# Causal attention block: softmax sums by additions of the weighting exponentials, maxima from high parts alone

## What is computed

```
x = x + 0.5 * (LN(x) @ sign_weight^T * scale + bias)        # feed-forward, ternary weights
x = x + softmax_causal(K Q^T / sqrt(32)) V @ Wo + bo        # 16 heads of 32, on LN(x)
x = x + 0.5 * (LN(x) @ sign_weight^T * scale + bias)        # feed-forward again
```

## Time and profile before

| | us |
|---|---|
| median of 3 runs | 1121.8 (1120.65 to 1125.34) |
| the profiled execution | 1119.35 |
| its span | 1117.6 |
| PE busy in the span | 1069.2 |
| ACT, DVE, POOL busy | 921.3, 738.3, 343.9 |
| granted TensorE clock, mean | 0.984 of full |

### The profile page before, as it was taken

The page is one execution under the profiler, slowest core; times in us unless marked ns, Lnnn a source line. Parts: engine busy times, 40 slices in busy tenths (PEclk is TensorE's granted clock), DMA queues, the critical chain, the costliest instruction groups (busy, mean ns, idle before and its releaser), DMA issues.

```text
span 1117.6 us, 26124 instructions
## 1 busy us (share of the span) xinstructions
PE 1069.2 (96%) x9472; PEld 692.7 (62%) x9472; DVE 738.3 (66%) x2306; ACT 921.3 (82%) x2577; POOL 343.9 (31%) x471
## 2 busy tenths in 40 slices
PE   5799999999999999999999999999999999999896
PEld 3576655565666665666666666665666666664465
DVE  6866577787535766889645776789744676755344
ACT  2269998999989989879988988878988988989641
POOL 3841232233002413445201323435301332300343
PEclk8898999999999999999999999999999999999899
DMA  6463211021104120421113211421112211000111
GB/s 203 155 217 124 96 50 40 3 78 50 34 8 154 31 68 30 152 69 50 37 34 107 68 48 50 143 78 46 44 40 86 73 63 50 22 21 12 42 65 38
DMA packets 42015, 77.71 MB, mean 70 GB/s; under 512 B 5536, under 2 KB 11680, under 8 KB 41888
## 3 DMA queue, kind: packets, MB, share of 16 engines
q1 hardware_dynamic: 41888, 76.04, 20.4%
HBM read 49.81 MB, written 25.17 MB: 67 GB/s over the span
## 4 chain that ended last, share of the span: by engine, by line
PE 77%; ACT 12%; DVE 5%; POOL 2%; issue 2%; DMA 1%; SPq 0%; ACTq 0%; DVEq 0%; POOLq 0%
PE bank L1134 31%; PE bank L1255 10%; PE bank L1193 10%; PE bank L1227 10%; PE bank L1156 8%; ACT masked_scores L1034 7%; ACT prob L1060 4%; PE bank L1145 3%; PE bank L1235 3%; DVE st L820 1%; DVE masked_scores L870 1%; POOL xt L730 1%; DMA xt<-in_L_attn_x_dram 1%; PE bank L1208 1%; DVE hn L839 1%
## 5 line engine op out<-in xcount | busy, mean ns | idle before, releaser
L870 DVE CUSTOM_DVE_ANT_0 masked_scores<-bank,mask 128x512 f32<-128x512 f32 (+3 forms) x768 | 379.6, 554 | 222.1 <-PE bank L1193 221.0
L1034 ACT ACTIVATE masked_scores<-masked_scores,mst 128x512 f32<-128x512 f32 (+3 forms) x768 | 467.5, 619 | 2.0 <-DVE mst L870 2.0
L1060 ACT ACTIVATE prob<-bank 128x512 f32<-128x512 f32 (+1 forms) x640 | 301.7, 558 | 58.0 <-PE bank L1235 56.9
L769 POOL TENSOR_SCALAR_AFFINE_SELECT prob<-prob 128x512 f32<-128x512 f32 (+1 forms) x96 | 78.6, 819 | 365.5 <-ACT prob L1060 364.8
L1134 PE MATMUL bank<-hT,wqk 128*128 128x512 f32 x768 | 190.5, 397 | 0.0
L1227 PE MATMUL bank<-qT,kT 32*128 32x512 f32 (+2 forms) x2304 | 173.0, 376 | 4.9 <-DVE mst L870 1.9
L1193 PEld LDWEIGHTS bank<-kT,qT 32*128 32x128 f32 x2304 | 94.7, 184 | 117.1 <-issue 52.4
L1193 PE MATMUL bank<-kT,qT 32*128 32x512 f32 (+2 forms) x2304 | 161.9, 376 | 4.7 <-ACT prob L1060 3.8
L1134 PEld LDWEIGHTS bank<-hT,wqk 128*128 128x128 f32 x768 | 140.6, 188 | 36.9 <-ACT prob L1060 7.2
L1034 ACT ACTIVATION_READ_ACCUMULATOR masked_scores<-masked_scores,mst 128x1 f32 x768 | 155.8, 203 | 0.0
L1227 PEld LDWEIGHTS bank<-qT,kT 32*128 32x128 f32 x2304 | 99.5, 184 | 72.0 <-issue 47.0
(11 more groups left out here) (87 smaller groups left out, 971.2 us busy)
## 6 DMA issues: line engine op xcount, KB each, us to landing
wqk<-weight_scratch SPq DMA_DIRECT2D x30, 512.0 KB, 3.3
wvo<-weight_scratch SPq DMA_DIRECT2D x20, 512.0 KB, 5.9
xt<-in_L_attn_x_dram SPq DMA_DIRECT2D x32, 256.0 KB, 4.2
residual_scratch<-xt SPq DMA_DIRECT2D x32, 256.0 KB, 2.0
xt<-residual_scratch SPq DMA_DIRECT2D x32, 256.0 KB, 2.9
out_dram<-xt SPq DMA_DIRECT2D x32, 256.0 KB, 2.0
o<-in_L_attn_Wqkv_dram SPq DMA_DIRECT2D x12, 256.0 KB, 5.2
weight_scratch<-o SPq DMA_DIRECT2D x6, 512.0 KB, 3.0
```

The source lines that it names most:

```text
L769: nc.gpsimd.affine_select(out=part, in_=part, compare_op=ALU.is_ge, fill=0.0, base=0, pattern=[[0, 4], [0, m], [1, P]], channel_multiplier ...
L870: nc.vector.tensor_tensor_reduce(masked_scores[:, h, at:at + n], psum(u, h)[:, at:at + n], mask[:, off:off + n], -SCALE, BIG, ALU.add, ALU ...
L1034: nc.scalar.activation(of, of, ACT.Exp, bias=mst[:, c + kc, to:to + 1], scale=-1.0, accum_out=ssum[:, c + kc, to:to + 1]).then_inc(a_free, 1)
L1060: nc.scalar.activation(prob[:, at % 2, h, off:CW], psum(("S", b, n), h)[:, off:CW], ACT.Exp, scale=SCALE)\
```

## The change

Sums: the tiles of A are no longer exponentiated. The sum over keys comes from `prob` itself: in each chunk the `prob` of the first step stays where it is, and the `prob` of every later step is added to it, three heads by VectorE in one instruction and the fourth by GpSimd. At the chunk's end a float32 matmul of ones (128 x 32) by this sum, one for each head, gives the sums of all queries spread over the partitions; VectorE takes the reciprocal of that bank, 128 x 512, and multiplies. `prob` gets a third buffer. The use N, `rall`, `pick`, `ssum`, `msh`, L1034 and L1038 are gone. C moves from the slots 0 and 3 of a group to 1 and 4.

Maxima: A has the term HI x HI alone. Tiles without a mask are reduced by a plain `tensor_reduce`; those on the diagonal keep the custom instruction. M writes one fp32r row (ScalarE alone, one DMA), and the matmul with `mneg` has K = 1.

The core of the diff (tables of rows, declarations, removed bodies cut):

```diff
 GROUP0_ROWS = (
-    "C P | A | LO",
-    "N M P | A | X3.0",
+    "P | A | LO",
+    "C M P | A | X3.0",
     "P | A | X3.1",
-    "C O.0 | A | X3.2",
-    "O.1 | A | X3.3",
-    "N T3.0 O.2 | A",
+    "O.0 | A | X3.2",
+    "C O.1 | A | X3.3",
+    "T3.0 O.2 | A",
...
     def uses(self):
-        return self.blocks + self.whole
+        sums = [u for u in self.whole if u[0] == "C"]
+        return sums + self.blocks + [u for u in self.whole if u[0] != "C"]
...
-        prob = sb("prob", [P, 2, 4, CW])
+        prob = sb("prob", [P, NPROB, 4, CW])          # NPROB = 3
...
+        def additions(n, heads):
+            c, keys = step_of(n % STEPS)
+            for j, kb in enumerate(keys):
+                off = first_query(c, kb)
+                yield (prob[:, HOME[chunk_first(n)], heads, off:CW],
+                       prob[:, HOME[n], heads, off - HALF * j:CW - HALF * j])
...
         def _(sp):
             def rows(u):
                 _, b, g, c = u
-                sp.wait_ge(ring_free, freed(u))
-                for part in (HI, LO):
-                    sp.dma_start(mneg[part:P:HD, c, :]..., mrow[:, c, part, :]...).then_inc(mrow_in[c], 16)
-            def inverse_rows(u):
...
+                sp.wait_ge(row_done, ROWS[u] + 1)
+                sp.dma_start(mneg[0:P:HD, c, :]..., mrow[:, c, :]...).then_inc(mrow_in[c], 16)
...
         def _(pool):
+            def add(n):                                # at the start of slot n + 1, ahead of affine_select
+                f = chunk_first(n)
+                if n == f:
+                    return
+                if diagonal(n % STEPS):
+                    pool.wait_ge(masked, diagonals(n))
+                else:
+                    pool.wait_ge(s_exp, 4 * n + 4)
+                pool.wait_ge(value_done, f + 1)
+                for j, (to, of) in enumerate(additions(n, slice(3, 4))):
+                    if ADDED[n - 1]:
+                        pool.wait_ge(added_pool, ADDED[n - 1] + j)
+                    nc.gpsimd.tensor_tensor(to, to, of, ALU.add).then_inc(added_pool, 1)
...
         def _(dve):
             def maximum(u):
...
+                        if kc < c:
+                            i = nc.vector.tensor_reduce(to, of, AX, ALU.max)
+                        else:
+                            i = nc.vector.tensor_tensor_reduce(masked_scores[:, h % 2, at:at + n], of, mask[:, off:off + n], 1.0, -BIG,
+                                                               ALU.add, ALU.max, to)
...
+            def add(n):                                # first in slot n + 1
...
+                for j, (to, of) in enumerate(additions(n, slice(0, 3))):
+                    if ADDED[n - 1]:
+                        dve.wait_ge(added, ADDED[n - 1] + j)
+                    nc.vector.tensor_tensor(to, to, of, ALU.add).then_inc(added, 1)
...
             def scaled(u):
                 _, b, g, c = u
-                dve.wait_ge(accv_free, ended(u) + 1)
                 dve.wait_ge(ring_full, full(u))
+                nc.vector.reciprocal(inverse[:, :], psum(u)).then_inc(inverse_done, 1)
+                dve.wait_ge(inverse_done, ended(u) + 1)
+                dve.wait_ge(accv_free, ended(u) + 1)
                 of = chunk(b, CHUNKS * g + c)
-                nc.vector.tensor_tensor(of, psum(u), of, ALU.mult).then_inc(ring_free, 1)
+                nc.vector.tensor_tensor(of, of, inverse[:, :], ALU.mult).then_inc(ring_free, 1)
...
         def _(act):
-            def block_sums(u, heads):
...
+            def row(u):
+                act.wait_ge(ring_full, full(u))
+                nc.scalar.activation(mrow[:, u[3], :], psum(u)[0:4 * QPC, 0:P], ACT.Identity, scale=-1.0).then_inc(row_done, 1)
...
             def exponentials(b, n):
                 off = live(n % STEPS)
                 at = step(b, n)
+                held = [m for m in range(at) if HOME[m] == HOME[at]][-1:]
+                for m in held:
+                    if chunk_first(m) == m:
+                        i = m % STEPS
+                        act.wait_ge(ring_full, full(("C", m // NSTEP, m % NSTEP // STEPS, 1 if i else 0)))
+                    else:
+                        act.wait_ge(value_done, m + 1)
+                        act.wait_ge(added, ADDED[m])
+                        act.wait_ge(added_pool, ADDED[m])
...
         def _(pe):
                 elif kind == "A":
...
-                    for term, (x, y) in enumerate(((HI, HI), (LO, HI), (HI, LO))):
-                        for j, r, at, keys, _ in block_tiles(u):
+                    for j, r, at, keys, _ in block_tiles(u):
...
                 elif kind == "C":
-                    pe.wait_ge(pick_set, 3)
-                    pe.wait_ge(rall_in, 32 * (ended(u) + 1))
-                    nc.tensor.matmul(psum(u), pick[:, :], rall[:, :], start=True, stop=True).then_inc(ring_full, 1)
+                    n = last_step(u)
+                    pe.wait_ge(added, ADDED[n])
+                    pe.wait_ge(added_pool, ADDED[n])
+                    for h in range(4):
+                        m = nc.tensor.matmul(psum(u)[HD * h:HD * h + HD, :], ones[:, 0:HD], prob[:, HOME[chunk_first(n)], h, :],
+                                             start=True, stop=True)
+                    m.then_inc(ring_full, 1)
...
-                    pe.wait_ge(mrow_in[c], 32 * group(b, g))
+                    pe.wait_ge(mrow_in[c], 16 * group(b, g))
```

More of the change, by code:

```diff
@@ L1 @@
+import itertools
 from contextlib import ExitStack
@@ L322, with homes, chunk_first @@
 RING = 7
+NPROB = 3
+def homes():
+    free, at, total = [0] * NPROB, [], None
+    for n in range(B * NSTEP):
+        first = step_of(n % STEPS)[1][0] == 0
+        here = min(range(NPROB), key=lambda m: free[m])
+        assert free[here] <= n
+        if first and total is not None:
+            free[total] = n + 2
+        if first:
+            total = here
+        free[here] = B * NSTEP + NPROB if first else n + 2
+        at.append(here)
+    return at
+HOME = homes()
+def chunk_first(n):
+    i = n % STEPS
+    return n - i + (0 if i < CHUNK_STEPS[0] else CHUNK_STEPS[0])
+ADDED = list(itertools.accumulate(len(step_of(n % STEPS)[1]) - (chunk_first(n) == n) for n in range(B * NSTEP)))
 XLOADS = [("X1", 0, t) for t in range(NX)] + [w for s in SLOTS for w in s.loads if w[0] in ("X1", "X3")]
@@ L350, in use @@
                 self.full[u] = full
-            if u[0] not in ("A", "V") and u not in [TURNED[n] for n in BY_ACT]:
+            if u[0] not in ("A", "V", "M") and u not in [TURNED[n] for n in BY_ACT]:
                 self.freed[u] = freed
@@ L763, in _ @@
                     i = s.step % STEPS
+                    n = step(s.b, s.step)
+                    if n:
+                        add(n - 1)
                     if diagonal(i):
[L765 removed]
                         at, m = live(i), len(step_of(i)[1])
[L767 removed]
+                        part = prob[:, HOME[n], :, at:at + m * P].rearrange("p h (m q) -> p h m q", m=m)
                         pool.wait_ge(s_exp, 4 * n + 4)
@@ L889, in inverse @@
-            def inverse(u):
-                _, b, g, c = u
-                if c == 0:
-                    dve.wait_ge(a_free, block_at(maxima(b, g, 0)[-1]))
-                else:
-                    dve.wait_ge(inverse_done, 4 * group(b, g) - 1)
-                if ended(u):
-                    dve.wait_ge(ring_full, full(("N", b, g, c - 1) if c else ("N", *before(b, g), 1)))
-                nc.vector.reciprocal(rcol[:, :], msh[:, 0, :] if c else ssum[:, 0, :]).then_inc(inverse_done, 1)
+                    nc.vector.tensor_tensor(mcol[:, :], mst[:, 1, :], mst[:, 2, :], ALU.max).then_inc(mcol_done, 1)
@@ L942, in _ @@
                     first_stats(k)
-                for u in s.uses():
-                    if u[0] == "N":
-                        inverse(u)
-                    elif u[0] == "C" and u[3] == 0:
-                        combine(u)
+                if s.step is not None and step(s.b, s.step):
+                    add(step(s.b, s.step) - 1)
+                elif (s.b, s.row) == (B, 0):
+                    add(B * NSTEP - 1)
                 if s.step is None and k > 1:
@@ L1082, in _ @@
                         high_output(u)
-                for u in s.blocks:
-                    block_sums(u, range(4) if u != s.blocks[-1] else range(3))
                 for u in s.uses():
```

231 lines of the change are left out of this document (92 added, 139 removed).

## The result

| | us |
|---|---|
| before, median of 4 | 1121.2 |
| changed kernel, median of 3 | 1258.8 (1252.2 to 1265.4) |
| ratio | 1.1227, 95% interval 1.1183 to 1.1271 |
| forecast | 1162, range 1108 to 1198 |

A forecast was written before the change was run, and what follows sets the result against it. TensorE was taken as the bound in most groups, with VectorE second. Batches 0 to 2 +9, +13, +14, batch 3 +5, −3, tail +8, head −5: +41 us, counted from between profiled run and median, 1162 us; range 1108 to 1198.

The forecast's parts named there:

- Group 2 of batches 1 and 2: Groups forecast to be longest, near 80 us, with VectorE at 79.3 us against TensorE's 60.8 in batch 1.
- a group takes what its fuller engine has: Each group's time was set to the larger of VectorE's busy time + 18.8 us and TensorE's − 6.6.
- unevenness: Slots with C get 4.5 + 1.7 us more VectorE work; costed at about 2 us a group, 8 a batch.
- Its own sign of being wrong: A stretch with neither engine full, meaning a wait through `prob`, the sums or GpSimd's queue, costed at nothing.
- the last stretch: Last group and tail, without A: two reciprocals in the open before the output projection, +8 us, bounds 3 and 12.
- rival 4: TensorE's clock drops to 0.93 throughout, as in the tail: at most +20 us, mostly hidden; no chance of its own.
- group 2 of batch 3: Bound by ScalarE at 53.2 us before, it was to become 48.5 + 2, a change of −3 us.
- TensorE's saving on A: A loses two of three terms; of its matmuls' 9.43 us a group, 6.3 us were to go.
- the 0.133 us of L1255: Price taken for each of C's float32 matmuls of 512 columns: 8 a group, 1.07 us.
- The reciprocal's price: VectorE's 128 x 512 reciprocal at 8 ns an element: 4.2 us each, two a group, 8.4 us.
- the lower bound: Lower near bound for the reciprocal: the floor hides exactly 32 elements, giving 6.1 ns an element.
- Rival 2: VectorE's and GpSimd's additions hold each other up: 46 us, some 35 where VectorE is the bound; 1197 us, chance 0.15.

The follow-up runs named there:

- e5_logs: Changed kernel with C's reciprocal moved to ScalarE as exp(-ln(sum)), VectorE only multiplying: 1266.2 us, ratio 1.129.
- e11_alone: Kernel before, plus a 128 x 512 reciprocal of spare data ahead of the maxima in each of the 32 slots with C: 1180.3 us, ratio 1.052.
- e10_pieces: Changed kernel, ScalarE copying C's bank to SBUF, the reciprocal cut into four 128-column pieces at the ends of four slots: 1218.2 us, ratio 1.084.
- e3_late: Changed kernel, ScalarE copying C's bank to SBUF, VectorE's reciprocal and multiplication moved to the end of the slot: 1272.0 us, ratio 1.134.
- e4_filler: Changed kernel, TensorE doing A's matmuls six times over in slots with C, same operands and results: 1234.8 us, ratio 1.100.
- e6_maxima: Kernel before with A cut to the term HI x HI, for its sums as for its maxima, all else unchanged: 1096.8 us, ratio 0.979.
- e8_noadd: Changed kernel without the additions on VectorE and GpSimd, so softmax sums are left out: 1197.9 us, ratio 1.069.
- e9_nopool: Changed kernel without GpSimd's additions alone, so every fourth head's sum is left out: 1246.4 us, ratio 1.112.
- e2: Changed kernel, ScalarE copying C's bank to SBUF, VectorE taking the reciprocal of the copy at the same place in its queue: 1280.8 us, ratio 1.143.

## Why the prediction was right and wrong

**Right:** the sign, and that the bound passes from TensorE towards VectorE. VectorE's busy time (1039 worked out, 1026.6 measured), in part by luck: the additions took 223 us where the forecast had 190, the reciprocals 107 where it had 134. Group 2 of batches 1 and 2 (79.3 + 2 forecast, 84.0 and 82.3 measured). ScalarE out of the picture (475 us). The reciprocal costs far more an element than an addition.

**The step that failed** is the rule "a group takes what its fuller engine has", with 2 us a group for unevenness. It treats the two engines as if each could work ahead. The groups where it failed are those in which neither is full: groups 0 and 3 of batch 1 were to take 60.3 and 59.3 us, and 2 for unevenness, and took 69.2 and 70.5. A block of 3.4 to 6 us of VectorE work, or waiting, between two sets of maxima costs time whatever VectorE's average; e5_logs (107 us less load, same time), e11_alone (29% of VectorE idle, +59 us) and e10_pieces against e3_late (same work, −54 us) show it. The forecast had seen that slots with C get 4.5 + 1.7 us more, and priced it as unevenness. Its own sign of being wrong came true, a stretch in which neither engine is full, but the wait went through the banks and the maxima, not through `prob`, the sums or GpSimd's queue. In the last stretch the forecast had 8 us more, with bounds of 3 and 12, and it took 17 more.

**The clock**, rival 4, was bounded at +20 us, "mostly hidden". Its rough loss went from 18 to 94 us. The mechanism was named and the size was off, because I took it that the kernel would be evenly loose, as the tail was. It is not: the clock falls in stretches, behind most of the long gaps and behind some short ones, and where TensorE has least to do it is lowest: 0.86 in group 0 of batch 0, and 0.70 in group 2 of batch 3, which was to gain 3 us and took 62.4 for 53.2. In e4_filler a part of that loss is gone and the time falls by 24 us, the added matmuls included.

**Two terms of the sum were mis-sized.** TensorE's saving on A: a third of the matmuls was to cost a third of the time; it cost 93 of 162 us. In e6_maxima, with no wide reciprocal and no additions about, A's 512-wide matmuls take 59.2 us for 384, 0.154 each, so this belongs to short runs of matmuls and not to the stalls. A block of A of the same shape in the kernel before and in e6_maxima, each with the instruction behind it:

```profile
647.18 0.98 PE L1193 MATMUL bank<-kT,qT 32*128 32x256 f32 x24
648.10 0.66 PE L1145 MATMUL bank<-ident,hn 128*128 128x128 f32 x4
```

```profile
654.23 0.51 PE L1193 MATMUL bank<-kT,qT 32*128 32x256 f32 x8
654.67 0.28 PE L1208 MATMUL bank<-ident,rcol 128*16 128x128 f32 x1
```

Three terms hold TensorE for 0.92 us, one term for 0.44. So a term is worth 0.24 us and each block keeps some 0.2 us that doesn't depend on the number of terms (worked out from these two rows): two of three terms gone are half of the block's time, and not two thirds. And C: in the rows each float32 matmul stands twice (L1237 is x256 for 128 in the program), so the 0.133 us of L1255 was half a matmul's price: 36 us instead of 17 (16 x 1.07).

**The reciprocal's price:** 3.35 us, 4.2 taken, 3.3 the lower bound. (3354 − 241) / (512 − 16) = 6.3 ns an element, which leaves a fixed part of 0.14 us: the floor hides just the 32 elements of the lower bound. The Trainium skill's repeat count of 8 (VectorE: DVE Perf Modes, "First, the fixed hardware budget"), read as 8 cycles of 0.96 GHz an element, gives an estimate of 8.3 ns; the trace has 6.3, and the measurement decides.

**Rival 2**, the hold between VectorE and GpSimd, is real and, as far as the runs show, cheap. A 1536-wide addition takes 1928 ns on the mean, where the median one takes 1759, and GpSimd's smallest instruction is the one that suffers:

```profile
L740 POOL TENSOR_SCALAR ve<-mv 128x1 f32<-128x1 f32 x96 | 81.0, 844 | 103.5 <-DVE mv L864 100.4
```

It took 202 ns before, and 205 in e8_noadd, without the additions. The Trainium skill (SBUF — State Buffer, "Who interferes with whom") describes this hold for an instruction's whole length, and the 1.5 to 1.7 us that 35 of the 96 take, each of them beside a VectorE addition, agree. But in e9_nopool, with GpSimd's additions gone, VectorE's wide ones still take 1868 ns (GpSimd's other work stays) and the time falls by about 12 us, not the 35 of the rival. What the slower GpSimd instruction costs by itself no run shows; VectorE waits for the result that hangs on it (L743) for 6.5 us in the whole kernel. Two of the rival's inputs were off: the 1.52 us of the earlier trace rows belong to a form that takes 1356 ns on the mean in that trace, not 1286, and the additions and multiplications are 192, not 176.

What could have shown it beforehand is VectorE's wait for A's matmuls in the kernel before (us, times, longest):

```profile
DVE masked_scores L870 <- PE bank L1193: 221.0, 133, 6.0
```

That is 1.7 us each time. Read as the time by which the maxima can be late before others feel it, it leaves 1.6 us of a reciprocal of 3.3, and e11_alone measured 1.8; the mean fits, but no run shows it for single slots.

**Open:** where the 22 and 13 us of e2 and e3 above the changed kernel come from, how much GpSimd's additions cost, how much of the 138 us is clock and how much is waiting, and what the clock falls behind when the gap is short.

## What to carry to other kernels

Where two engines hand each other banks with little lead, compare the longest block of one engine between two hand-overs with the wait that the trace shows there, not sums of busy time over a stage. Here a slow instruction was better cut up and spread (54 us) than moved within its slot or given to another engine with the same delay (no gain). And test the parts of a change one at a time: here one part makes the kernel before 2% faster, and is worth less than half of that behind the other.

## What was not expected of the hardware

A reciprocal of 128 x 512 takes 3.35 us, 6.3 ns an element, six times an addition's. A gap of 3.1 us in TensorE's work was followed by a stretch at a granted clock of 0.61, in which a product took 4.42 us for 3.01; 860 more matmuls in the slots with such gaps made the kernel faster by 24 us. Alternating logarithm and exponential on ScalarE loaded a table each time, 64 loads of 1283 ns. Matmuls over 32 rows and 512 columns, in four strips, cost 0.15 us each in runs of 4 and 0.089 in runs of 12. A GpSimd instruction of one element a partition took 844 ns on the mean for 202, once VectorE made wide additions.
